# A gated cross-attention block with routed experts on one core: norms on GpSimd in wide operations, x resident from the load on, output bias added by TensorE

## Chip, core and metric

The kernel runs on 1 core of one Trainium2 chip. The metric is the device time in microseconds (us) of one execution. Engines: TensorE (PE, with its weight loads as PEld), VectorE (DVE), ScalarE (ACT), GpSimd (POOL), SyncE (SP, which issues DMAs). Each has its own instruction stream; streams meet only through semaphores, on which an engine waits in its own order.

## The reference

`x` and `ctx` are 128 batches of 64 tokens of 128 channels, all float32. Cut to what matters:

```python
def reference(x, ctx, g_xattn, g_ffn, W_q, b_q, W_k, b_k, W_v, b_v, W_o, b_o, w_red, wg, W1, b1, W2, b2):
    # xattn: 16 heads of 8 channels; softmax(q k^T / sqrt(8)) v, then @ W_o + b_o
    x = x + tanh(g_xattn[0]) * xattn(layernorm(x), ctx, ctx, ...)
    # ffn: 8 experts, hidden 256. logits = (h @ w_red) @ normed(wg).T; the expert
    # with the largest gate alone does gelu(h @ W1 + b1) @ W2 + b2, times its gate
    x = x + tanh(g_ffn[0]) * ffn(layernorm(x), w_red, wg, W1, b1, W2, b2)
    return x
```

`layernorm` has neither scale nor shift, eps is 1e-5.

## The kernel before

**Tiles.** The 8192 tokens are 64 units of 128 tokens (two batches). Four units make a step `s` (`CU` = 4, `NC` = 16 steps). The attention is one loop of 76 slots `k` (`SLOTS` = 64 + `LAGO`, `LAGO` = 12), which every engine walks in the same order of slots; slot `k` belongs to step `k // 4` at place `j = k % 4`. A unit passes through the slots with lags: its scores for the row maxima 4 slots behind (`LAG1`: L1121 on TensorE, then the two maxima, L976, on VectorE), the scores from which the exponentials are taken at lag 10 (`LAG2`: L1104 and L1111, then ScalarE's L596 and L598), sums and values at lag 11 (`LAGV`: L1184 and L1191), reciprocal (L982) and scaled rows (L993) on VectorE, and the output projection at lag 12 (L1195), added to the residual by L988. So in one slot TensorE does L1104, L1111, L1121, L1184, L1191, L1195, each for another unit.

**Once a step** TensorE turns the normed rows (L1263, `j` = 0) and the context (L1216, `j` = 0), makes keys (L1223, `j` = 1), queries (L1281, `j` = 2) and values (L1288, `j` = 3), and a product for the routing logits (L1207, `j` = 3). ScalarE copies each out of PSUM (L557 to L638). SyncE spreads keys and queries over partitions (L298, L305) and loads the context two steps and x three steps ahead (`next_loads`).

**x and the residual.** `XR` holds one record of 144 columns for each token: 128 of x (`X` is that part), 8 routing logits, the mean (`R_MEAN`), then 1/deviation (`R_RSTD`), gate (`R_GATE`) and row number (`R_ID`). x comes into three buffers `XC`. VectorE takes its statistics (L708, L716) into `mv`; `ve` is the variance plus eps. The output bias, tanh(gate) x (b_o + b_v W_o), is made in `bias_row` (VectorE, slot 2) as a row `tgbo` on all partitions, with its mean `bmean`. GpSimd writes x + `tgbo` into `X` (L367, `with_bias`), and mean + `bmean` into the record. What the bias does to the logits is `clog`, added for each group of units in `route_peak` (L809).

**GpSimd's step** has this order (L449 to L464): `spread` (L443, waits for ScalarE's turned maxima), records to send `before`, `norm` of step s+1 (power of -0.5 in `deviation`, L352; deviation, L360; four L375, one a unit; `with_bias`), `gate_norm` of step s-4 (L384, power L386, into the record), records to send `behind`. The power is taken for four columns at a time, once for each of the two norms. Steps 0 and 1 are normed by VectorE (L729), with the power on GpSimd.

**Routing** goes by `GROUPS` of units (12, 12, 12, 8, 8, 4, 4, 4). `route_slots` sets the slots of a group's six parts on VectorE; among them is the count on TensorE (L1158, L1161: one product with all columns of the group, then one for each unit with 8 columns fewer each time), and `route_place`, which waits for GpSimd's gate norm (`g_pay`). Records then go by indirect DMA (`send`, L400) to a table in HBM, sorted by expert; the number a step is written out in `sends`.

**Experts.** 71 tiles of 128 records: load (L320), norm (L948), turn (L1228), first product (L1236), gelu (L584), second product with its bias as a bfloat16 product over an exact three-part split (L1323, then L1326), gate and residual (L1037), and a scatter to the output by GpSimd (L471). The last group's four records are sent after the sixth scatter.

**Setup touched by the change.** `setup_gate` waits for `tgbo`; `setup_turn` turns it (L1083) and `setup_logits` makes from it `clog`, copied by ScalarE in `output_logits` (L550, L551) at slot 10; TensorE waits for `wox_ok` at slot 11. `split_biases` (L791 to L795) splits the experts' bias on VectorE at slot 10.

## Time and profile before

| what | before |
|---|---|
| time of three runs | 377.30, 378.38, 379.06 us, median 378.38 |
| span of the profiled execution | 376.4 us (first to last instruction); its own time is not listed apart, and stands as this span and what lies around it |
| PE / PEld busy | 332.6 us (88%) / 261.4 us (69%) |
| DVE / ACT / POOL busy | 290.0 us (77%) / 242.3 us (64%) / 266.9 us (71%) |
| chain that ended last | PE 62%, issue 9%, POOL 9%, DVE 8%, ACT 6% |
| mean granted TensorE clock | 0.963 of full speed |
| HBM | 17.13 MB read, 10.04 MB written, 72 GB/s |

Busy time is that in which an engine worked, waits left out. Matmuls are pipelined and their ends are modelled, so starts are the better guide on TensorE. Spans on POOL are rough. The chain is followed back from the last instruction to what released each step. The attention is over at about 265 us, the experts fill the rest.

### The profile page before, as it was taken

To read this page: it belongs to the slowest core of one execution; us is meant where nothing else is said; L and a number is where in the kernel's file an instruction comes from. 1 tells how busy PE (TensorE), PEld (TensorE's weight loads), DVE (VectorE), ACT (ScalarE), POOL (GpSimd) and SP (SyncE) were. 2 spreads that over 40 slices of the span, in tenths; PEclk is the share of its full clock that TensorE was granted. 3 is DMA by queue.
4 is the path that set the end of the run, shared out by engine and by line. 5 is a ranking of instruction groups with operands and counts; after the bars stand their busy time and mean duration, and the time that the engine had idled before them with its cause. 6 is when DMAs were issued, how large, how long until landed. Compare 5 with 4: busy or idle time off the path is not lost.

```text
span 376.4 us, 17275 instructions
## 1 busy us (share of the span) xinstructions
PE 332.6 (88%) x6654; PEld 261.4 (69%) x6654; DVE 290.0 (77%) x900; ACT 242.3 (64%) x604; POOL 266.9 (71%) x349
## 2 busy tenths in 40 slices
PE   3878999999999999999999997776888999999960
PEld 1534776776776777876876866655776899999950
DVE  7777788889899898989899799966578666666630
ACT  3747688788788788788788885644443455555520
POOL 6494664474685898798796876787557777777771
PEclk9978999999999999999999999997699999999995
DMA  5344334323313423323211121143014433333210
GB/s 114 105 141 141 102 95 129 111 80 98 118 48 98 139 80 105 95 70 102 71 63 51 44 93 50 41 129 97 36 56 132 137 120 99 114 110 100 66 46 0
DMA packets 47164, 34.13 MB, mean 91 GB/s; under 512 B 9800, under 2 KB 42955, under 8 KB 47083
## 3 DMA queue, kind: packets, MB, share of 16 engines
q1 hardware_dynamic: 42440, 23.90, 22.6%
q0 software_dynamic: 4352, 9.00, 6.6%
q8 instruction: 54, 0.88, 1.0%
q14 instruction: 26, 0.21, 0.2%
q10 hardware_dynamic: 292, 0.13, 0.1%
HBM read 17.13 MB, written 10.04 MB: 72 GB/s over the span
## 4 chain that ended last, share of the span: by engine, by line
PE 62%; issue 9%; POOL 9%; DVE 8%; ACT 6%; SPq 2%; DMA 1%; POOLq 0%; DVEq 0%; ACTq 0%
PE m L1326 10%; PE sc L1236 8%; PE pv L1184 7%; POOL records L400 6%; PE pv L1191 5%; PE sc L1111 5%; PE pv L1195 5%; PE m L1288 4%; PE sc L1121 3%; PE sc L1104 3%; PE sc L1228 2%; PE m L1323 2%; ACT PT L598 1%; PE m L1263 1%; PE m L1216 1%
## 5 line engine op out<-in xcount | busy, mean ns | idle before, releaser
L976 DVE TENSOR_REDUCE mx<-sc 128x8 f32<-128x512 f32 x128 | 82.2, 684 | 20.7 <-PE sc L1121 20.2
L471 POOL DMA_INDIRECT out<-fo,rr x71 | 70.0, 986 | 23.3 <-issue 19.3
L400 POOL DMA_INDIRECT records<-XR,pos x64 | 63.4, 991 | 20.4 <-issue 16.4
L982 DVE RECIPROCAL rec<-pv 128x128 f32<-128x128 f32 x64 | 61.1, 954 | 10.4 <-PE pv L1195 5.2
L596 ACT ACTIVATE PT<-sc 128x512 f32<-128x512 f32 x64 | 38.1, 595 | 28.2 <-issue 20.1
L1326 PE MATMUL m<-w,fgT 128*128 x284 | 50.7, 302 | 0.1
L1236 PE MATMUL sc<-fxT,w1s 128*128 128x128 f32 x284 | 45.6, 284 | 4.2 <-DVE w1s L964 3.3
L1037 DVE SCALAR_TENSOR_TENSOR fo<-m,rr 128x128 f32<-128x128 f32 x71 | 24.9, 350 | 29.8 <-PE m L1326 29.8
L1184 PE MATMUL pv<-PT,kz 128*32 128x128 f32 x1024 | 41.7, 281 | 6.5 <-DVE XR L988 5.9
L375 POOL TENSOR_SCALAR xn<-XC,mv,rstd 128x128 f32<-128x128 f32 x56 | 44.2, 799 | 0.0
L1236 PEld LDWEIGHTS sc<-fxT,w1s 128*128 128x128 f32 x284 | 38.6, 197 | 6.5 <-ACT fxT L578 4.2
L578 ACT ACTIVATE fxT<-sc 128x128 f32<-128x128 f32 x71 | 19.7, 278 | 35.4 <-PE sc L1228 35.4
L1191 PE MATMUL pv<-PT,V 128*32 128x64 f32 x2048 | 41.3, 220 | 0.2 <-issue 0.2
L1326 PEld LDWEIGHTS m<-w,fgT 128*128 128x128 f32 x284 | 38.0, 194 | 2.6 <-issue 0.4
L1111 PE MATMUL sc<-Qd,kT 32*128 32x128 f32 x1024 | 39.8, 270 | 0.0
L584 ACT ACTIVATE fgT<-sc 128x256 f32<-128x256 f32 x71 | 27.3, 384 | 18.7 <-PE sc L1236 18.3
L598 ACT ACTIVATE PT<-sc 128x512 f32<-128x512 f32 x64 | 38.3, 598 | 0.0
L1191 PEld LDWEIGHTS pv<-PT,V 128*32 128x32 f32 x2048 | 37.6, 111 | 0.3 <-issue 0.3
L1184 PEld LDWEIGHTS pv<-PT,kz 128*32 128x32 f32 x1024 | 24.5, 109 | 14.5 <-DVE XR L988 7.2
L1111 PEld LDWEIGHTS sc<-Qd,kT 32*128 32x128 f32 x1024 | 34.4, 186 | 0.0
L1195 PE MATMUL pv<-wox,OT 128*128 128x137 f32 x128 | 32.5, 336 | 0.0
L352 POOL TENSOR_TENSOR rstd<-ve,mhalf 128x4 f32<-128x4 f32 x16 | 16.5, 1034 | 21.6 <-DVE ve L721 21.4
(207 smaller groups left out, 681.3 us busy)
## 6 DMA issues: line engine op xcount, KB each, us to landing
rr<-records SPq DMA_DIRECT2D x71, 72.0 KB, 2.0
XC<-in_x SPq DMA_DIRECT2D x16, 256.0 KB, 3.2
C<-in_ctx SPq DMA_DIRECT2D x16, 256.0 KB, 3.1
Qd<-Qf SPq DMA_DIRECT2D x64, 64.0 KB
Kd<-kb SPq DMA_DIRECT2D x64, 32.0 KB
w<-in_L_ffn_W SPq DMA_DIRECT2D x16, 128.0 KB, 2.8
out<-fo,rr POOLq DMA_INDIRECT x71, 2.3
w1l<-in_L_ffn_W SPq DMA_DIRECT2D x8, 128.0 KB, 3.3
```

Source lines behind the costliest of these rows:

```text
L375: i = nc.gpsimd.tensor_scalar(xn[:, u, :], XC[c % 3][:, u, :], mv[c % 2][:, u, 0:1], rstd[:, u:u + 1], ALU.subtract, ALU.mult)
L400: nc.gpsimd.indirect_dma_start(out=records, out_offset=bass.IndirectOffsetOnAxis(ap=pos[:, u:u + 1], axis=0), in_=XR[:, u, :], in_offset=N ...
L471: nc.gpsimd.indirect_dma_start(out=out_rows, out_offset=bass.IndirectOffsetOnAxis(ap=rr[q][:, R_ID:R_ID + 1].bitcast(U32), axis=0), in_=fo ...
L598: nc.scalar.activation(pt[:, 2:4], sc[:, 2:4, 256:512], ACT.Exp).then_inc(pt_ok, 1)
L976: nc.vector.tensor_reduce(mx[c % 2][:, t:t + 2, HI * u:HI * u + HI], sc[:, t:t + 2, 0:256].rearrange("p t (i k) -> p t i k", i=HI), AX_X, ...
L982: nc.vector.reciprocal(rec[:, :], pv[:, P:2 * P]).then_inc(rec_ok, 1)
L1111: m = nc.tensor.matmul(sc[:, t, 256 + P * b:256 + P * b + P].rearrange("p (i q) -> p i q", i=2), kT[c % 3][r, u, b, :, :].rearrange("r l k ...
L1184: nc.tensor.matmul(pv[32 * t:32 * t + 32, P:2 * P].rearrange("p (b q) -> p b q", b=2), kz[:, 16 - 16 * i:48 - 16 * i], PT[n % 2][:, HI * t ...
L1191: last = nc.tensor.matmul(pv[32 * t:32 * t + 32, S * b:S * b + S], vf[:, at:at + 32], PT[n % 2][:, HI * t + 2 * b + i, :], start=False, st ...
L1195: last = nc.tensor.matmul(pv[:, 2 * P:2 * P + DX], OT[no % 2][:, :], wox[:, :], start=True, stop=True, skip_group_check=True)
L1236: i = nc.tensor.matmul(sc[:, 2 + p, P * m:P * m + P], w1s[p][:, P * m:P * m + P], fxT[p][:, :], start=True, stop=True, skip_group_check=True)
L1326: i = nc.tensor.matmul(o, fgT[p][:, m, :], w2[:, bass.ds(e, 1), m, :].rearrange("p o c -> p (o c)"), start=False, stop=(m == HH - 1), skip ...
```

## The change

- x is loaded straight into `X`; the buffers `XC` go, and statistics go straight into the record (`R_MEAN` and the column behind it).
- GpSimd's norm is two operations over all four units (subtract the mean, times 1/deviation) in place of four; `with_bias` and the two writes of the mean go.
- From step 4 on the two powers of a step are one over 8 columns (`roots`), ahead of the norm; the gate's result is copied into the record by an operation of its own. It now waits for the squares before the norm. In the last four steps, which have no norm, `roots` still takes a power and a copy.
- The bias is no longer added to x. `box` has 137 columns: the bias row and what it adds to the logits and the mean. VectorE splits it at slot 10 (`bias_parts`, behind ScalarE's `wox_ok`) into three bfloat16 rows at partitions 0, 32 and 64, and TensorE adds it with a bfloat16 product of 128 weights and 137 columns ahead of each L1195 (64 of them).
- `route_peak` loses the addition of `clog`; `bias_row` loses three of its four operations; SyncE's wait for `xb_ok` goes.

```diff
             def load_x(c):
-                sp.dma_start(XC[c % 3][:, :, :], x_t[:, CU * c:CU * c + CU]).then_inc(x_in[c % 3], 16)
+                sp.dma_start(X[:, CU * c:CU * c + CU, :], x_t[:, CU * c:CU * c + CU]).then_inc(x_in[c % 3], 16)
...
                 if s + 3 < NC:
                     sp.wait_ge(xn_ok, s + 1)
-                    sp.wait_ge(xb_ok, s + 1)
                     load_x(s + 3)
...
+            def root(c):
+                pool.wait_ge(ve_ok, c + 1)
+                nc.gpsimd.tensor_tensor(rstd, ve, mhalf[:, 0, :], ALU.pow).then_inc(rstd_ok, 1)
+
+            def roots(c, g):
+                pool.wait_ge(gsq_ok, CU * g + CU)
+                nc.gpsimd.tensor_scalar(gve, gsq[g % 2][:, :], 1.0 / D, EPS, ALU.mult, ALU.add).then_inc(gve_ok, 1)
+                if c is not None:
+                    pool.wait_ge(ve_ok, c + 1)
+                pool.wait_ge(gve_ok, g + 1)
+                if c is None:
+                    nc.gpsimd.tensor_tensor(inv[:, 1, :], gve, mhalf[:, 1, :], ALU.pow).then_inc(ginv_ok, 1)
+                else:
+                    nc.gpsimd.tensor_tensor(inv[:, :, :], both[:, :, :], mhalf[:, :, :], ALU.pow).then_inc(rstd_ok, 1)
+                    pool.wait_ge(rstd_ok, c + 1)
+                if c is None:
+                    pool.wait_ge(ginv_ok, g - (NC - 5) + 1)
+                nc.gpsimd.tensor_copy(XR[:, CU * g:CU * g + CU, R_RSTD], inv[:, 1, :]).then_inc(g_pay, 1)
...
             def norm(c):
+                r = slice(CU * c, CU * c + CU)
+                nc.gpsimd.tensor_tensor(xc[:, :, :], X[:, r, :], XR[:, r, R_MEAN:R_MEAN + 1].to_broadcast([P, CU, D]),
+                                        ALU.subtract).then_inc(xc_ok, 1)
                 deviation(c)
                 pool.wait_ge(xT_ps, c)
-                for u in range(CU):
-                    i = nc.gpsimd.tensor_scalar(xn[:, u, :], XC[c % 3][:, u, :], mv[c % 2][:, u, 0:1], rstd[:, u:u + 1],
-                                                ALU.subtract, ALU.mult)
-                i.then_inc(xn_ok, 1)
-                with_bias(c)
+                pool.wait_ge(xc_ok, c - 1)
+                nc.gpsimd.tensor_tensor(xn[:, :, :], xc[:, :, :], per_unit(rstd), ALU.mult).then_inc(xn_ok, 1)
...
                 if before:
                     send(sent, sent + before)
+                if s + 1 < NC and 1 <= s < 4:
+                    root(s + 1)
+                if s >= 4:
+                    roots(s + 1 if s + 1 < NC else None, s - 4)
                 if 2 <= s + 1 < NC:
                     norm(s + 1)
                 if s == 2:
                     constants()
-                if s >= 4:
-                    gate_norm(s - 4)
...
             def bias_row():
                 dve.wait_ge(bvo_ps, 1)
-                link(nc.vector.tensor_tensor(tgbo[:, :], m2[:, 128:128 + D], bo[:, :], ALU.add))
+                nc.vector.tensor_tensor(box[:, 0:D], m2[:, 128:128 + D], bo[:, :], ALU.add).then_inc(box_ok, 1)
                 dve.wait_ge(tg_ok, 1)
-                link(nc.vector.tensor_scalar(tgbo[:, :], tgbo[:, :], tg[:, 0:1], None, ALU.mult))
-                link(nc.vector.tensor_reduce(bmean[:, 0:1], tgbo[:, :], AX_X, ALU.add))
-                nc.vector.tensor_scalar_mul(bmean[:, 1:2], bmean[:, 0:1], 1.0 / D).then_inc(tgbo_ok, 1)
+
+            def bias_parts():
+                dve.wait_ge(wox_ok, 1)
+                link(nc.vector.tensor_copy(bpart[:, 0, :], box[:, :]))
+                link(nc.vector.tensor_tensor(brest[:, 0, :], box[:, :], bpart[:, 0, :], ALU.subtract))
+                link(nc.vector.tensor_copy(bpart[:, 1, :], brest[:, 0, :]))
+                link(nc.vector.tensor_tensor(brest[:, 1, :], brest[:, 0, :], bpart[:, 1, :], ALU.subtract))
+                link(nc.vector.tensor_copy(b3[:, :], brest[:, 1, :]))
+                link(nc.vector.memset(pick3[:, :].bitcast(U32), 0))
+                for r in range(3):
+                    i = nc.vector.memset(pick3[32 * r:32 * r + 1, :], 1.0)
+                i.then_inc(pick3_ok, 1)
+                for r in range(2):
+                    i = nc.vector.tensor_copy(b3[32 * r:32 * r + 32, :], bpart[32 * r:32 * r + 32, r, :])
+                i.then_inc(b3_ok, 1)
...
                 if k == 10:
                     split_biases()
+                    bias_parts()
...
-                link(nc.vector.tensor_tensor(e_, XR[:, f:l, D:D + NE], per_expert(clog[:, 0:NE], m), ALU.add))
-                nc.vector.tensor_reduce(c_[:, 0], e_, AX_X, ALU.max).then_inc(peak_ok, 1)
+                nc.vector.tensor_reduce(c_[:, 0], XR[:, f:l, D:D + NE], AX_X, ALU.max).then_inc(peak_ok, 1)
...
                 if 0 <= no < NU:
-                    last = nc.tensor.matmul(pv[:, 2 * P:2 * P + DX], OT[no % 2][:, :], wox[:, :], start=True, stop=True,
+                    if no == 0:
+                        pe.wait_ge(b3_ok, 1)
+                        pe.wait_ge(pick3_ok, 1)
+                    nc.tensor.matmul(pv[:, 2 * P:2 * P + DX], pick3[:, :], b3[:, :], start=True, stop=False,
+                                     skip_group_check=True)
+                    last = nc.tensor.matmul(pv[:, 2 * P:2 * P + DX], OT[no % 2][:, :], wox[:, :], start=False, stop=True,
                                             skip_group_check=True)
```

## Rows read from the trace of the kernel before

**Rows 1.** Busy time by stage: stretch, length, PE, PEld, DVE, ACT, POOL, clock, DMA.

```profile
60.00:200.00 140.00, 138.10 (x3663) 103.92 (x3651) 123.83 (x339) 116.37 (x271) 105.44 (x135) 1.00 0.31 92
220.00:258.00 38.00, 29.00 (x883) 22.80 (x881) 32.03 (x111) 22.26 (x61) 28.17 (x33) 1.00 0.29 86
```

**Rows 2.** Timeline, all engines (start, length, engine): L1263 of two steps, one ScalarE wait.

```profile
43.02 0.60 PE L1263 MATMUL m<-ident,xn 128*128 128x128 f32 x4
...
191.38 0.61 ACT L598 ACTIVATE PT<-sc 128x512 f32<-128x512 f32 x1
...
192.10 0.10 PEld L1104 LDWEIGHTS sc<-MD,usel 32*128 32x128 bf16 x4 [0.76 <-ACT PT L598]
...
198.18 0.60 PE L1263 MATMUL m<-ident,xn 128*128 128x128 f32 x4
```

**Rows 3.** Timeline of GpSimd in the expert stage: first record after the sixth scatter, last scatter.

```profile
280.01 0.96 POOL L400 DMA_INDIRECT records<-XR,pos  x1 [2.32 <-DVE XR L863]
...
367.69 0.98 POOL L471 DMA_INDIRECT out<-fo,rr  x1 [0.30 <-issue]
```

**Rows 4.** Timeline of TensorE in two second slots of a step; last, a group.

```profile
46.48 1.02 PE L1223 MATMUL m<-cT,wkp 128*128 128x512 f32 x2
...
47.44 0.29 PE L1104 MATMUL sc<-MD,usel 32*128 32x256 bf16 x4
...
187.21 0.50 PE L1195 MATMUL pv<-wox,OT 128*128 128x137 f32 x2
...
187.55 1.02 PE L1223 MATMUL m<-cT,wkp 128*128 128x512 f32 x2
...
188.45 0.50 PE L1161 MATMUL m<-oh,ones 128*128 128x96 bf16 x12
...
188.88 0.29 PE L1104 MATMUL sc<-MD,usel 32*128 32x256 bf16 x4
...
L1323 PE MATMUL m<-b2s,pick 128*128 x71 | 16.2, 227 | 0.1
```

**Rows 5.** Groups of GpSimd: out<-in, shapes, count | busy us, mean ns | idle before.

```profile
L375 POOL TENSOR_SCALAR xn<-XC,mv,rstd 128x128 f32<-128x128 f32 x56 | 44.2, 799 | 0.0
L367 POOL TENSOR_TENSOR XR<-XC,tgbo 128x512 f32<-128x512 f32 x16 | 20.3, 1270 | 0.0
...
L352 POOL TENSOR_TENSOR rstd<-ve,mhalf 128x4 f32<-128x4 f32 x16 | 16.5, 1034 | 21.6 <-DVE ve L721 21.4
...
L408 POOL TENSOR_TENSOR nrm<-nrm 8x1 f32<-8x1 f32 x1 | 1.5, 1481 | 1.1 <-DVE nrm L746 1.1
...
L354 POOL COPY XR<-mv 128x4 f32<-128x4 f32 x2 | 0.4, 192 | 0.0
```

**Rows 6.** Timeline at the end of the attention, and the stretch behind it.

```profile
253.13 0.19 DVE L809 TENSOR_TENSOR ex<-XR,clog 128x32 f32<-128x32 f32 x1
...
256.83 0.19 DVE L849 TENSOR_TENSOR ex<-ex,XR 128x32 f32<-128x32 f32 x1 [0.52 <-POOL XR L386]
...
259.48 1.08 PE L1184 MATMUL pv<-PT,kz 128*32 128x128 f32 x16 [2.17 <-DVE XR L988]
...
260.00:280.00 20.00, 17.35 (x144) 14.94 (x136) 12.65 (x51) 7.49 (x25) 11.62 (x13) 0.76 0.13 44
```

**Rows 7.** Timeline of VectorE, the bias row in slot 2: first and last of three.

```profile
17.67 0.29 DVE L754 TENSOR_SCALAR tgbo<-tgbo,tg 128x128 f32<-128x128 f32 x1
...
18.31 0.15 DVE L756 TENSOR_SCALAR bmean<-bmean 128x1 f32<-128x1 f32 x1
```

**Rows 8.** Timeline of slots 10 to 12: what the new split stands between.

```profile
37.33 0.20 ACT L551 ACTIVATE wox<-pv 128x9 f32<-128x9 f32 x1
37.35 1.29 DVE L976 TENSOR_REDUCE mx<-sc 128x8 f32<-128x512 f32 x2
...
38.67 0.60 ACT L598 ACTIVATE PT<-sc 128x512 f32<-128x512 f32 x1
...
39.95 0.29 PE L1104 MATMUL sc<-MD,usel 32*128 32x256 bf16 x4
...
41.42 0.32 PE L1121 MATMUL sc<-Kd,qb 32*64 32x256 bf16 x8 [0.73 <-issue]
```

91 lines of the change are left out of this document (34 added, 57 removed).

## The prediction

> **What bounds the kernel now.** I read busy time by stage first [rows 1], then one step of four units in order of time [rows 2], then the last stage. The reader should see three stages.
>
> From 60 to 200 us TensorE is busy 138.10 of 140 us at full clock (2.4 GHz), while VectorE has 16 us to spare and GpSimd 35 us [rows 1]. A step lasts (198.18 - 43.02) / 11 = 14.1 us [rows 2]. One place in a step is not TensorE's alone: at 192.10 the load of L1104 starts 0.11 us after ScalarE's second exponential ended (191.38 + 0.61), having waited 0.76 us for it, while the products of L1281 still ran [rows 2]. TensorE's 1.9 us of idle time in ten steps, 0.19 a step, is what such places leave.
>
> From 220 to 258 us there are no projections left. TensorE is busy 29.0 of 38 us and VectorE 32.0 [rows 1]. From about slot 69 on a loop sets the pace: values (TensorE), reciprocal and residual (VectorE), next values.
>
> In the expert stage GpSimd sets the end: from the last group's first record at 280.01 to the last scatter at 367.69 there are 4 records and 71 - 6 = 65 scatters, 87.7 us over 68 intervals, 1.29 us each, with only issue time between them [rows 3]. The change touches none of these. So whatever moves the start of the expert stage moves the end by as much.
>
> **The change, part by part.** The sum is made against the profiled execution, whose span is 376.4 us (the page's first line); the runs shown have 378.38 us as their median, 2.0 us more, and I add that at the end.
>
> *1. The bias product (TensorE), 64 instructions added.* Each unit gets a bfloat16 product, 128 weights by 137 columns, between L1191 and L1195. No row shows it there, so I bound it:
> - From below: the slot at 187.55 has a count (one product of 96 columns and twelve of 96 falling to 8, 720 columns in all) behind L1223, that at 46.48 has none. L1223 to L1104 takes 188.88 - 187.55 = 1.33 us against 47.44 - 46.48 = 0.96 us, so 13 products cost 0.37 us, 0.028 us each, or 0.51 ns a column [rows 4]. By the column, 137 columns cost 0.07 us; by the instruction alone 0.03 us. I take 0.03 as the end of the range.
> - From above: L1195 is a float32 product with the same 137 columns in two passes, 187.21 to 187.55, so 0.17 us a pass [rows 4]. The nearest relative is L1323, also bfloat16, 128 by 128, and followed by float32 products: 16.2 us over 71 is 0.228 us of overlapped duration [rows 4], which is no spacing; I take the pass's 0.17 as the end.
> I take 0.08 us, just over the price by the column, since that row has real bfloat16 weight loads, hidden as these should be. A negative price is excluded: nothing is taken off TensorE.
>
> Slots 12 to 63 make 13 steps. In each, the product of the slot that ends in the ScalarE wait is hidden by the 0.19 us above; three count: 39 x 0.08 = 3.1 us. Were that cover gone, 13 x 0.08 = 1.0 us more. In slots 64 to 69 VectorE sets the pace and covers it. In the last six the loop contains it: 6 x 0.08 = 0.5 us. Sum +3.6 us; ends 39 x 0.03 + 0.2 = 1.4 us and 52 x 0.17 = 8.8 us.
>
> *2. GpSimd.* Before, a step takes four L375 at 0.80, L367 at 1.27 and two powers at 1.03 [rows 5]: 6.5 us. After: two products of 128x512, both at L367's 1.27 us, one power of 128x8, and one small copy at 0.19, as L354 [rows 5]. The power of eight columns isn't shown: four columns take 1.03 us, and one column over 8 partitions took 1.48 us [rows 5], so it doesn't go by columns; I take 1.1 us, with 2.1 us (two old ones) as the other end. After is 3.8 us, 2.7 us a step less. It is worth nothing: GpSimd has 35 us to spare in those 140 us [rows 1]. Even at 2.1 us, and with the new wait for the squares of the gate's norm, which now stands ahead of the step's norm, the normed rows are needed only in the next step. Queued behind that new wait are the norm and the second batch of records; the waited-for squares belong to the step's first slot, over 10 us before TensorE needs the rows.
>
> In the last steps there is no norm left, and the separate copy into the record makes GpSimd slower, 0.2 to 0.3 us a step with its wait. There it matters once: at 256.83 VectorE waited 0.52 us for GpSimd's gate norm [rows 6]. Two copies lie ahead, +0.5 us, but VectorE's own slots are later by as much through part 1. I count 0.1.
>
> Here a rule speaks against the change. The rows show a one-input operation over 128 columns at 0.80 us and a two-input one over 512 at 1.27 us [rows 5]: wide wins, 2.5 us for 3.2. The Trainium skill (GPSIMD Engine Reference, Engine selection) has it that a one-input operation runs roughly at line rate on GpSimd, and a two-input one about twice as slow as on VectorE; by it the old norm would be the cheaper and GpSimd's load would not fall. The measured rows decide for me, and the sum is the same by either, since this work is covered.
>
> *3. VectorE.* The three operations of the bias row that go (L754 to L756, 17.67 to 18.46) lie on the way to the row maxima of the second unit: -0.8 us [rows 7]. Against that, splitting the bias comes at slot 10: five linked operations over 137 columns at about 0.29 us, as L754 [rows 7], then six small ones (between 0 and 6 x 0.29; I take 0.7): 2.2 us. It must wait for ScalarE's L551 (37.33 + 0.20), which falls just at the time the maxima of slot 11 started (37.35) [rows 8]. Those move by 2.4 us. Behind them stand ScalarE's exponentials, which ended at 38.67 + 0.60 and would now end at 41.7, and TensorE's slot 12, which started at 39.95 and so is 1.7 us late; 0.73 us of it disappears in the wait that L1121 had at 41.42 [rows 8]. So +0.9 us; ends 0 and 2.4. The addition of the logits' constant goes from each group; three of these lie in the stage where VectorE paces, -0.19 each [rows 6], of which two count: -0.4 us.
>
> *4. Loads.* x goes straight into the resident rows, in pieces of the same 512 bytes; SyncE loses one wait, for rows that TensorE doesn't need yet: 0. What covers it is the three steps of lead.
>
> **Sum.** +3.6 (product) + 0.1 (copy) - 0.8 + 0.9 - 0.4 = +3.4 us: span 379.8, time 381.8 us. A difference under 0.5% (1.9 us) is about what a measurement of this kernel can't tell from no change; the limits are 376.5 and 380.3 us.
>
> **The rivals.**
> - *The product nearly disappears* (0.03 us as the short ones, more cover than I count). For: a weight load can run beside the product before it, as L1104's does [rows 2], and 13 products cost 0.37 us [rows 4]. Against: those were short. 39 x 0.03 + 0.2 = 1.4, and the other terms at -0.2: +1.2 us, 379.6 us. Chance 0.22.
> - *The product costs more* (0.12 us) and the setup's stall counts fully. 39 x 0.12 + 6 x 0.12 = 5.4 us, with the stall at its end of 2.4 (+0.1 - 0.8 + 2.4 - 0.4 = +1.3): +6.7 us, 385.1 us. For: the float32 product behind it must load its weights beside a shorter one. Against: twelve loads of 128 weights among the count's products cost no more than their columns [rows 4]. Chance 0.18.
> - *Faster: TensorE's clock stays up at the change of stage.* Place: slots 73 to 75, where L1184 waited 2.17 us for VectorE at 259.48, and the granted clock then fell to half (1.2 GHz). Its mean over 260 to 280 us is 0.76, which makes 20 x 0.24 x 2 = 9.6 us at half clock [rows 6]. If this idle time is broken up, TensorE, busy 17.35 of those 20 us, gets back at most 9.6 x 0.87 / 2 = 4.1 us. It decides only if the rest of the sum is under 4.1 - 1.9 = 2.2 us, so with the cheap product: 378.4 + 1.2 - 4.1 = 375.5 us. Against: the wait comes from GpSimd's late gate norm and register loads, which the change doesn't shorten. Chance 0.08. The same clock can also fall once more, at slot 11, where TensorE now idles 1.7 us longer; that belongs to the case before.
> - *It doesn't do what it says*, GpSimd isn't relieved (the power takes 2.1 us, broadcast operands are slow). Then POOL rows show it and the time doesn't, being covered. No chance of its own.
>
> **How the numbers follow.** Forecast as summed 0.52; cheap product 0.22 (within 0.5%); dear product 0.18; clock 0.08 (faster). Slower: 0.52 + 0.18 = 0.70, same 0.22, faster 0.08. The range from 377.8 to 385.5 us takes in the cheap product and most of the dear one, and leaves out the clock's case and the far end of 8.8 us. The likeliest case's own range is 380.3 to 383.5 us.
>
> **What would show it.** Right: the period of a step, by the starts of L1263, goes from 14.1 to 14.3 or 14.4 us; TensorE still over 98% busy from 60 to 200 us; the new product's start lies 0.08 us before L1195's; GpSimd's busy time falls by some 40 us with nothing gained; the maxima of slot 11 start 2 us later; from the last group's records to the end 87.7 us as before. Wrong: a step still of 14.1 us (then the product is free), a step under 14 us (then something I hold for covered was on the path), or a clock row near 1.0 between 260 and 270 us.

## The result, and the profile of the changed kernel

The changed kernel takes 385.98 us (median of 4 runs, 384.15 to 388.53), the kernel before beside it 378.53 us (377.30 to 379.06). The ratio is 1.0216, 95% interval 1.0161 to 1.0271: slower, by 7.5 us where the prediction had 3.4 us, and 385.98 lies just above its range, which ended at 385.5. The profiled execution has a span of 384.9 us against 376.4, so 8.5 us are to be found. The ratios leave out executions more than 1.5% above the fastest of their kernel, mostly those of the variants in the fourth set of experiments below (nine of 24 of two of them) and of the kernel before in the fifth (ten of 17), so there the medians of all executions stand beside them.

First the busy time by stage, the answer to [rows 1] and to the stretch of [rows 6] (columns as there).

```profile
60.00:200.00 140.00, 135.62 (x3580) 102.69 (x3580) 122.85 (x322) 112.64 (x262) 71.35 (x89) 0.99 0.31 93
220.00:258.00 38.00, 32.94 (x973) 26.00 (x966) 33.01 (x102) 25.45 (x66) 25.98 (x32) 1.00 0.18 61
260.00:280.00 20.00, 14.35 (x289) 11.80 (x281) 13.04 (x48) 10.31 (x31) 15.12 (x19) 0.91 0.30 88
```

GpSimd has its relief: 71.35 us of 140 in place of 105.44. TensorE, which sets the pace there, is not busier but idler: 135.62 us in place of 138.10. A product that cost much would have kept it busy. So something makes it wait. (The later stretches lie some 10 us earlier in the work than those of the kernel before.)

Next the start of the steps, by the first transpose of each (L1279, before L1263). This table takes both traces' timelines of TensorE; the lengths are those of the stretch that ends with this start (so the expectations below count steps), and the last column shows where the time goes.

| start of step | before, us | after, us | length up to it, before | the same, after | later than before |
|---|---|---|---|---|---|
| 2 | 28.79 | 28.52 | 12.27 | 11.63 | -0.27 |
| 3 | 43.02 | 48.06 | 14.23 | 19.54 | +5.04 |
| 7 | 99.16 | 104.58 | 14.04 | 14.10 | +5.42 |
| 8 | 113.25 | 121.39 | 14.09 | 16.81 | +8.14 |
| 9 | 127.36 | 136.53 | 14.11 | 15.14 | +9.17 |
| 11 | 155.94 | 165.84 | 14.54 | 15.09 | +9.90 |
| 14 | 198.18 | 209.12 | 14.09 | 15.09 | +10.94 |
| 15 | 212.78 | 223.50 | 14.60 | 14.38 | +10.72 |

Most lengths are 14.09 or 14.10 us, 0.06 more than the 14.03 or 14.04 of before. The loss comes in a few lumps: 5.3 us up to the start of step 3, 2.7 up to step 8, 1.0 up to steps 9 and 14, and 0.6 up to step 11. At the end it is 8.5 us, so 2.2 us are gained back behind the start of step 15.

**The first lump.** The timelines of VectorE, of GpSimd and of TensorE in slots 10 to 12 of the changed kernel, the answer to [rows 8].

```profile
35.88 2.81 DVE L803 CAST bhl<-bw 128x8 bf16<-128x8 f32 x1
38.72 0.17 DVE L804 TENSOR_TENSOR br<-bw,bhl 128x8 f32<-128x8 f32 x1
...
39.42 0.38 DVE L757 CAST bpart<-box 128x137 bf16<-128x137 f32 x1
...
41.35 0.62 DVE L764 MEMSET pick<- 1x128 bf16 x3
42.01 0.40 DVE L767 COPY b<-bpart 32x137 bf16<-32x137 bf16 x2
42.43 1.29 DVE L987 TENSOR_REDUCE mx<-sc 128x8 f32<-128x512 f32 x2
```

```profile
35.84 1.04 POOL L388 TENSOR_TENSOR xn<-xc,inv 128x512 f32<-128x512 f32 x1
36.81 0.20 POOL L415 MEMSET tri<- 128x128 bf16 x1
...
38.56 0.10 POOL L423 MEMSET ebase<- 128x1 f32 x1
38.61 0.16 POOL L424 IOTA tile_i<- 128x36 int32 x1
```

```profile
44.41 0.29 PE L1115 MATMUL sc<-MD,usel 32*128 32x256 bf16 x4 [4.30 <-ACT PT L600]
```

The maxima of slot 11 start at 42.43 in place of 37.35. Of the 5.1 us, 3.0 are the new pieces of the bias (39.42 to 42.41). The rest comes from the first copy of the *old* split of the expert biases: eight columns to bfloat16, 2.81 us, where the same copy took 0.15 us before; the four instructions behind it are 0.7 us shorter in sum than they were beside the old norm. It starts 0.04 us behind GpSimd's second wide product of the norm, and ends at 38.69, when the last of GpSimd's 22 memsets (38.56 + 0.10) is over. Nothing that it reads is late. Behind it TensorE waits 4.30 us for ScalarE, and the granted clock then falls to half (1.2 GHz) for a while: its mean is 0.72 over 44 to 50 us, 1.00 before. So the 5.3 us hold the wait and the slow stretch behind it.

**The second lump.** VectorE and GpSimd where group 0 is placed.

```profile
113.41 0.86 DVE L856 TENSOR_TENSOR ky<-ky,oh 128x96 f32<-128x96 f32 x1
114.30 0.25 DVE L858 TENSOR_REDUCE pos<-ky 128x12 uint32<-128x96 f32 x1
114.47 2.13 DVE L860 TENSOR_TENSOR ex<-ex,XR 128x96 f32<-128x96 f32 x1
116.52 1.27 DVE L987 TENSOR_REDUCE mx<-sc 128x8 f32<-128x512 f32 x2
```

```profile
113.11 1.04 POOL L388 TENSOR_TENSOR xn<-xc,inv 128x512 f32<-128x512 f32 x1
114.11 2.38 POOL L394 TENSOR_TENSOR w<-w,w1l 128x1024 f32<-128x1024 f32 x1
```

Both routing instructions read two tiles in SBUF. They took 0.26 and 0.25 us before; here one ends just behind GpSimd's product (114.27 and 114.15), and the other with its subtraction on w1 at 116.5. The reduction between them, with one tile, keeps its 0.25 us. TensorE then waits 1.95 us for ScalarE, until 118.48, and the clock is 0.72 over 119 to 125 us, which is the lump up to step 9. Those up to steps 11 and 14 hold the same pair of instructions at 0.91 and 0.97 us, beside the norm alone.

What did the kernel before do at that hour? These are its rows, with the norm in its old form:

```profile
107.94 0.26 DVE L845 TENSOR_TENSOR ky<-ky,oh 128x96 f32<-128x96 f32 x1
...
108.40 0.25 DVE L849 TENSOR_TENSOR ex<-ex,XR 128x96 f32<-128x96 f32 x1
```

```profile
106.07 3.24 POOL L375 TENSOR_SCALAR xn<-XC,mv,rstd 128x128 f32<-128x128 f32 x4
...
111.83 2.38 POOL L392 TENSOR_TENSOR w<-w,w1l 128x1024 f32<-128x1024 f32 x1
```

They stood beside GpSimd's norm then too, and lost nothing; the subtraction came 3 us behind them. None of the routing's two-tile instructions (L818, L828, L845, L849) fell beside a GpSimd instruction of 512 or more columns in that trace. This gives **theory G**: GpSimd's work was covered as far as its own deadlines go, but it holds up VectorE's instructions of some forms while it runs, and the change gave it new forms and new hours. Within it, **theory W** says that the form of the norm matters and not only the hour. **Theory P** is the prediction's: the products, and the split's own time, make the loss. The Trainium skill ("SBUF — State Buffer", Who interferes with whom) has a rule for G: a VectorE instruction with two SBUF inputs contends with a GpSimd instruction that reads SBUF, as does a copy or cast in a two-port mode, and whoever comes first holds the shared pair for its whole instruction. L860 beside L394 agrees with it to 0.1 us; it is weighed once more below.

**GpSimd's groups**, the answer to [rows 5].

```profile
L366 POOL TENSOR_TENSOR inv<-both,mhalf 128x8 f32<-128x8 f32 x11 | 18.2, 1657 | 14.8 <-DVE both L720 13.9
L383 POOL TENSOR_TENSOR xc<-XR 128x512 f32<-128x512 f32 x14 | 14.6, 1043 | 0.0
L388 POOL TENSOR_TENSOR xn<-xc,inv 128x512 f32<-128x512 f32 x14 | 14.6, 1039 | 0.0
...
L370 POOL COPY XR<-inv 128x4 f32<-128x4 f32 x16 | 3.0, 189 | 1.0
```

**The product** in the changed kernel, between the values (L1202) and the output projection, the answer to [rows 4]:

```profile
185.78 0.62 PE L1202 MATMUL pv<-PT,V 128*32 128x64 f32 x31
186.34 0.23 PE L1209 MATMUL pv<-b,pick 128*128 128x137 bf16 x1
186.41 0.45 PE L1211 MATMUL pv<-wox,OT 128*128 128x137 f32 x2
```

**The end.** First record of the last group and last scatter, the answer to [rows 3]:

```profile
288.47 0.96 POOL L402 DMA_INDIRECT records<-XR,pos  x1 [1.48 <-DVE XR L874]
...
376.18 0.98 POOL L473 DMA_INDIRECT out<-fo,rr  x1 [0.30 <-issue]
```

376.18 - 288.47 = 87.7 us, as before.

### The profile page after: what moved, and what is told of

It is laid out like the page before. It is cut to its first block, busy times and chain, and to the rows that moved or that the text cites. A ratio compares the mean times of both kernels' runs of the same rounds, so it can differ in the third digit from the quotient of the medians.

```text
span 384.9 us, 17329 instructions
## 1 busy us (share of the span) xinstructions
PE 335.6 (87%) x6718; PEld 264.5 (69%) x6718; DVE 297.9 (77%) x900; ACT 242.7 (63%) x604; POOL 225.1 (58%) x292
## 4 chain that ended last, share of the span: by engine, by line
PE 56%; DVE 12%; issue 11%; POOL 9%; ACT 6%; SPq 2%; DMA 1%; POOLq 0%; DVEq 0%; ACTq 0%
PE m L1342 10%; PE sc L1252 8%; POOL records L402 6%; PE pv L1195 6%; PE pv L1202 5%; PE sc L1122 5%; PE pv L1211 3%; PE sc L1132 3%; PE m L1304 3%; PE sc L1115 2%; DVE mx L987 2%; PE m L1339 2%; PE sc L1244 2%; PE m L1279 2%; PE m L1232 2%
## 5 line engine op out<-in xcount | busy, mean ns | idle before, releaser
L443 POOL TENSOR_TENSOR MD<-mS,imask 128x256 bf16<-128x256 bf16 x16 | 9.7, 608 | 76.8 <-ACT mS L647 76.8
L1195 PE MATMUL pv<-PT,kz 128*32 128x128 f32 x1024 | 42.4, 283 | 6.7 <-DVE XR L998 6.3
L1202 PE MATMUL pv<-PT,V 128*32 128x64 f32 x2048 | 42.1, 223 | 0.0
L1122 PE MATMUL sc<-Qd,kT 32*128 32x128 f32 x1024 | 39.8, 271 | 0.0
L1202 PEld LDWEIGHTS pv<-PT,V 128*32 128x32 f32 x2048 | 38.4, 113 | 0.1
L1195 PEld LDWEIGHTS pv<-PT,kz 128*32 128x32 f32 x1024 | 24.9, 110 | 15.1 <-DVE XR L998 7.3
L1115 PEld LDWEIGHTS sc<-MD,usel 32*128 32x128 bf16 x256 | 6.6, 91 | 39.1 <-ACT PT L600 26.4
L1115 PE MATMUL sc<-MD,usel 32*128 32x256 bf16 x256 | 18.4, 278 | 15.1 <-ACT PT L600 14.4
```

Of the source, the lines that this page charges most:

```text
L1115: nc.tensor.matmul(sc[:, t, 256:512].rearrange("p (b i q) -> p i b q", b=2, i=2), usel[r, u, :, :].rearrange("r l k -> r (l k)"), MD[c % 2 ...
L1122: m = nc.tensor.matmul(sc[:, t, 256 + P * b:256 + P * b + P].rearrange("p (i q) -> p i q", i=2), kT[c % 3][r, u, b, :, :].rearrange("r l k ...
L1195: nc.tensor.matmul(pv[32 * t:32 * t + 32, P:2 * P].rearrange("p (b q) -> p b q", b=2), kz[:, 16 - 16 * i:48 - 16 * i], PT[n % 2][:, HI * t ...
L1202: last = nc.tensor.matmul(pv[32 * t:32 * t + 32, S * b:S * b + S], vf[:, at:at + 32], PT[n % 2][:, HI * t + 2 * b + i, :], start=False, st ...
```

## The experiments

Eighteen runs were made, in five sets (the expectations call a set a "call"): the changed kernel itself twice, five repeats of other variants, and eleven more. The kernels of a set ran on one chip, beside the kernel before. **Two kinds of chip answered.** In two sets the kernel before took 377.5 and 378.3 us, with a clock of 0.96 in the profiled runs of the variants. In three it took 463.2, 464.5 and 467.6 us: there TensorE was granted 0.88 to 0.91, falling for long stretches from about 118 us on. On those the times say little, but the first 110 us of the traces, and the single instructions, read as elsewhere.

### First set: one part at a time (clock 0.88 to 0.91)

*No products.*

```diff
-                    nc.tensor.matmul(pv[:, 2 * P:2 * P + DX], pick3[:, :], b3[:, :], start=True, stop=False,
-                                     skip_group_check=True)
-                    last = nc.tensor.matmul(..., OT[no % 2][:, :], wox[:, :], start=False, stop=True,
+                    last = nc.tensor.matmul(..., OT[no % 2][:, :], wox[:, :], start=True, stop=True,
```

> The changed kernel with the bias product of each unit left out (64 small products fewer; the output bias and its logits are then missing from the result, all else stays). Theory P, the prediction's own: each product costs TensorE 0.06 to 0.08 us where it waits for nothing, so the kernel loses 3.5 to 4 us: 386.0 to about 382.3, ratio to the kernel before 1.010. Theory G, formed from the two traces (the slots of the changed kernel have the product in an opening that was already there; the loss lies in VectorE instructions held up while GpSimd works): about 0.02 us a unit, so -0.5 to -1.5 us, about 385, ratio 1.018; the step of four units goes from 14.09 to 14.03 us.

*Subtractions on w1 one step earlier.*

```diff
-                if 6 <= s < 8:
-                    fold_bias(s - 6)
+                if 5 <= s < 7:
+                    fold_bias(s - 5)
```

> The changed kernel with the two subtractions over half of w1 (GpSimd, 2.38 us each) one step earlier, in steps 5 and 6 in place of 6 and 7. Theory G: in the changed kernel the second of them runs at 114.1 to 116.5, over VectorE's routing instruction of group 0 that reads two tiles in SBUF, which takes 2.13 us there and 0.25 in the kernel before, and TensorE then waits 1.95 us and its clock falls; a step earlier no such instruction of VectorE is due. It expects that instruction below 1.0 us, no fall of the clock at 120 to 123 us and 2.5 to 3.5 us off the kernel: about 383, ratio 1.012. Theory P (the products and the split make the loss, GpSimd's work is covered): no change, within 0.5 us of the changed kernel, ratio 1.021.

*Constants one step later.*

```diff
-                if s == 2:
+                if s == 3:
                     constants()
```

> The changed kernel with GpSimd's constants (some 20 memsets and iotas, about 2.9 us) one step later, in step 3. Theory G: VectorE's first copy of the expert biases to bfloat16 in slot 10 takes 2.81 us because it starts while these memsets run back to back; without them beside it it takes 0.15 to 1.0 us (1.0 if it still starts within GpSimd's wide product of the norm), the maxima of slot 11 start at 39.8 to 40.6 in place of 42.43, and the kernel is 2 to 3 us shorter: about 383.5, ratio 1.013. Rival D (what is long there is the chain of bias pieces of VectorE itself, and the copy waits for data, the load of the expert biases): the copy ends at the same time, the maxima start at 42.4 and the time stays at 386, ratio 1.021.

*The norm in its old form.*

```diff
-                nc.gpsimd.tensor_tensor(xc[:, :, :], X[:, r, :], ..., ALU.subtract).then_inc(xc_ok, 1)
                 deviation(c)
                 pool.wait_ge(xT_ps, c)
-                pool.wait_ge(xc_ok, c - 1)
-                nc.gpsimd.tensor_tensor(xn[:, :, :], xc[:, :, :], per_unit(rstd), ALU.mult).then_inc(xn_ok, 1)
+                for u in range(CU):
+                    i = nc.gpsimd.tensor_scalar(xn[:, u, :], X[:, CU * c + u, :], XR[:, CU * c + u, R_MEAN:R_MEAN + 1],
+                                                rstd[:, u:u + 1], ALU.subtract, ALU.mult)
+                i.then_inc(xn_ok, 1)
```

> The changed kernel with the old form of the norm on GpSimd (four tensor_scalars of 0.80 us in place of two wide instructions of 1.04 us), all else as changed. Theory W (the form itself matters: instructions with two tiles in SBUF as inputs hold VectorE up, those with one tile and two columns do not): the routing instructions that took 0.8 to 1.0 us take 0.25 to 0.3 wherever only the norm ran beside them, and the kernel is 0.5 to 2 us shorter, about 385, though GpSimd works 1.1 us a step longer. Theory G without W (what counts is when GpSimd works, in either form): the long ones move to other places, time 385.5 to 387.5. Theory P: no change.

**Measured.** The kernel before took 463.19 us. The four took 470.40, 471.41, 470.03 and 471.45 us; ratios 1.0143 (1.0079 to 1.0208), 1.0164 (1.0101 to 1.0226), 1.0157 (1.0082 to 1.0232) and 1.0153 (1.0076 to 1.0230). By time they tell nothing apart: the interval of the first holds P's 1.010 and G's 1.018. By their rows they do:

- Without the products, the lengths up to steps 5, 6 and 7 are 14.03, 14.03 and 14.04 us; with them, where the subtractions or the constants were moved, 14.09 or 14.10. So a product costs 0.06 / 4 = 0.015 us, as G has it.
- With the subtractions moved, the routing instruction takes 0.25 us, and the length up to step 8 is 14.32 us in place of 16.81. The clock stays at 1.00 behind it, as G has it; but on such a chip it does so in the unedited changed kernel too, so that part is not shown here.
- With the constants moved, the first copy takes 1.02 us, and the maxima of slot 11 start at 39.79. G had 1.0 us and 39.8 to 40.6.
- With the norm in its old form, both routing instructions and the copy are short, though GpSimd's norm runs over them (113.20 to 116.33, and 35.22 to 38.34): W. But now the bias's second copy falls beside the memsets and takes 1.67 us, so the maxima of slot 11 start at 42.19 all the same.
- Rival D, that the first copy waits for its data, falls: with the constants moved it has ended by 36.24 us and with the old norm by 36.29, where the changed kernel's ended at 38.69.

Start times differ between runs by more than these gains, so the stall is better read as the distance from the maxima of slot 10 to those of slot 11. It is 3.03 us in the kernel before; 8.02 in the changed kernel, 6.37 and 7.24 in its two repeats below; 6.04 or 6.05 in all four runs with the constants moved and the pieces in slot 10; and 3.03 or 3.04 in the four below with the constants moved and the pieces elsewhere. So the pieces cost 3.0 us, and the copy held beside the memsets between 0.3 and 2.0 more. The distance is the same 6.05 in the two runs with only the constants moved, whether the first copy takes 1.02 us (here) or 0.25 (its repeat in the fourth set), since VectorE then waits 0.71 us for ScalarE's `wox`.

Timeline of VectorE in these kernels (subtractions moved; constants moved, then its repeat; old norm):

```profile
115.15 0.25 DVE L860 TENSOR_TENSOR ex<-ex,XR 128x96 f32<-128x96 f32 x1
```

```profile
35.22 1.02 DVE L803 CAST bhl<-bw 128x8 bf16<-128x8 f32 x1
...
39.79 1.29 DVE L987 TENSOR_REDUCE mx<-sc 128x8 f32<-128x512 f32 x2
```

```profile
37.29 0.25 DVE L803 CAST bhl<-bw 128x8 bf16<-128x8 f32 x1
...
39.07 0.23 DVE L757 CAST bpart<-box 128x137 bf16<-128x137 f32 x1 [0.71 <-ACT wox L553]
```

```profile
36.14 0.15 DVE L803 CAST bhl<-bw 128x8 bf16<-128x8 f32 x1
...
114.48 0.24 DVE L856 TENSOR_TENSOR ky<-ky,oh 128x96 f32<-128x96 f32 x1
...
114.93 0.38 DVE L860 TENSOR_TENSOR ex<-ex,XR 128x96 f32<-128x96 f32 x1
```

### Second set: the kernel unedited, the other direction, and sums (clock 0.89 to 0.91)

*The changed kernel again*, unedited:

> The changed kernel itself again, as the measure for the runs beside it, since the first four kernels ran on a chip that granted TensorE less clock (0.88 to 0.91 in place of 0.96) and took 467 to 474 us. Where the chip grants 0.96 again, every theory expects 386 us and a ratio to the kernel before of 1.021; where it grants 0.88, about 472 us and 1.016 to 1.021, by the ratios of 1.014 to 1.016 of its four variants there.

*The kernel before, with its split moved beside the memsets:*

```diff
-                if k == 10:
+                if k == 11:
                     split_biases()
```

> The kernel before with one edit: VectorE splits the expert biases in slot 11 in place of slot 10, so that the split falls beside GpSimd's memsets of the constants (39.37 to 42.3 us). Theory G (a copy of VectorE that starts beside GpSimd's work from SBUF or memsets waits for it): one of the split's five instructions takes 1 to 3 us in place of 0.15 to 0.38, the maxima of slot 12 start 1.5 to 3 us later than the 41.80 of the kernel before, and the kernel is 0 to 2.5 us longer, ratio 1.000 to 1.007. Theory P (the split costs its own 1.6 us wherever it stands, GpSimd's work is covered): each instruction keeps 0.15 to 0.38 us, ratio 1.000.

*Subtractions and constants both moved* (the two edits of the first set):

> The changed kernel with both moves of GpSimd's work that the first call looked at one by one: the constants one step later, the two subtractions on w1 one step earlier. Theory G: VectorE's first copy of the split takes 1.0 us in place of 2.8 and the routing instruction of group 0 takes 0.25 in place of 2.13 us; against the changed kernel beside it 3.5 to 6 us less, ratio to the kernel before 1.006 to 1.012. Theory P: the same time as the changed kernel.

*Everything but the constants:* old norm, subtractions moved, and VectorE's own pieces taken apart; `bias_parts` now takes the columns it works on.

```diff
+            link(nc.vector.memset(pick3[:, :].bitcast(U32), 0))      (behind norm(1), ahead of the slots)
...
+                if k == 4:
+                    bias_parts(slice(0, D), box_ok)
                 if k == 10:
-                    split_biases()
-                    bias_parts()
+                    bias_parts(slice(D, DX), wox_ok)
+                if k == 13:
+                    split_biases()
```

> The changed kernel with everything that theory G would do to it: the norm on GpSimd in its old form of four tensor_scalars with one tile as input (the one power a step stays), the subtractions on w1 one step earlier, the bias's first 128 columns split in slot 4 and only its 9 logit columns in slot 10, the selector written before the slots, the expert biases split in slot 13. Theory G: no instruction of VectorE in the routing above 0.5 us, the maxima of slot 11 at 37 to 38 us in place of 42.4, steps of 14.03 to 14.1 us; 7.5 to 10 us less than the changed kernel, ratio to the kernel before 0.995 to 1.002. Theory P (three to four of the lost microseconds are the products): ratio 1.007 to 1.012.

**Measured.** The kernel before took 464.54 us. The changed kernel: 470.76, ratio 1.0132 (1.0055 to 1.0208). The kernel before with its split moved: 466.75, 1.0008 (0.9969 to 1.0047). The two moves: 470.26, 1.0103 (1.0061 to 1.0145). Everything but the constants: 469.91, 1.0078 (1.0026 to 1.0130). The order is G's, but neighbours lie within each other's intervals, and the sizes are not G's: the two moves are 0.5 us under the changed kernel where G had 3.5 to 6, and the last one's ratio lies in P's range of 1.007 to 1.012 and above G's, which ended at 1.002.

The move in the kernel before is a miss for G. It expected one of the five instructions at 1 to 3 us; the first took 0.40 us in place of 0.15, though it stood in the row of memsets:

```profile
39.28 0.40 DVE L791 CAST bhl<-bw 128x8 bf16<-128x8 f32 x1
```

But later in the same run a thing happened that the kernel before had not shown: the routing instruction of group 2 fell beside its wide addition L367, and took 1.42 us, while its neighbour beside the norm took 0.34. VectorE, then GpSimd:

```profile
217.08 0.34 DVE L845 TENSOR_TENSOR ky<-ky,oh 128x96 f32<-128x96 f32 x1
...
217.63 1.42 DVE L849 TENSOR_TENSOR ex<-ex,XR 128x96 f32<-128x96 f32 x1
```

```profile
214.53 3.14 POOL L375 TENSOR_SCALAR xn<-XC,mv,rstd 128x128 f32<-128x128 f32 x4
217.64 1.26 POOL L367 TENSOR_TENSOR XR<-XC,tgbo 128x512 f32<-128x512 f32 x1
```

In groups 0 and 1 of this run the same instruction took 0.25 and 0.38 us beside the norm. So it is no matter of the changed kernel's code: in the kernel before, too, what GpSimd does beside it makes it long or short.

The short first copy shows that a copy beside the memsets need not wait for all of them. In the changed kernel's profile the same copy took 2.81 us, in its two repeats 1.31 and 2.02. What decides how soon it gets in is open. With it varies the first lump: step 4 starts at 62.3, 59.7 and 62.5 us in the three. And in the last of the four the nine logit columns were in the wrong place: in slot 10 they waited 1.69 us for ScalarE and then stood beside the constants, with one copy of nine columns at 1.85 us, so the maxima of slot 11 were no earlier (42.69):

```profile
39.58 0.18 DVE L761 CAST bpart<-box 128x9 bf16<-128x9 f32 x1 [1.69 <-ACT wox L553]
...
40.00 1.85 DVE L763 CAST bpart<-brest 128x9 bf16<-128x9 f32 x1
```

### Third set: the whole, on a chip at 0.96

*The changed kernel again:*

> The changed kernel itself once more, beside the three below. Two chips so far granted TensorE 0.88 to 0.91 and gave ratios of 1.013 (0.9055 clock). Every theory expects 1.021 where the chip grants 0.96 and 1.013 where it grants 0.90.

*All moves:* as the last one above, with the constants in step 3 and the nine columns in slot 11 in place of 10.

> The changed kernel with the norm of four tensor_scalars, the subtractions on w1 one step earlier, the constants one step later, the bias's first 128 columns split in slot 4, its 9 logit columns in slot 11, the expert biases in slot 13, the selector written before the slots. The last run of this kind had the 9 columns in slot 10, where VectorE waited 1.7 us for ScalarE and 1.85 us beside the constants. Theory G: no such wait is left, the maxima of slot 11 start at 36 to 37 us, the fourth step starts (first transposes) at 41 to 43 us against 44.7 to 48.1 in the changed kernel; at a clock of 0.96 the kernel takes 7.5 to 10 us less than the changed one (ratio to the kernel before 0.995 to 1.002), at 0.90 some 3 to 6 us less (1.000 to 1.006). Theory P: 1.008 to 1.012 at either clock.

*The same without the products:*

> The kernel above without the 64 bias products (output bias and its logits missing from the result). The pair prices the products with no stall of VectorE in the way. Theory G: a step is 14.03 in place of 14.09 us where the clock is whole, so the kernel is 0.5 to 1.5 us shorter than the one above. Theory P (0.06 to 0.08 us each): 3.5 to 4.5 us shorter, steps of 13.8 us or less against the one above.

*GpSimd's three moves alone* (old norm, subtractions earlier, constants later), VectorE as changed:

> The changed kernel with GpSimd's three moves alone (four tensor_scalars for the norm, subtractions on w1 one step earlier, constants one step later); VectorE's bias pieces stay in slot 10 as changed. Theory G: every routing instruction below 0.5 us and the expert bias copies at 0.15 us each, the maxima of slot 11 at 39 to 40 us because of the pieces' own 3.0 us, 1 to 2.5 us longer than the kernel with all moves. Theory P: the time of the changed kernel.

**Measured**, beside the kernel before at 377.47 us:

| kernel | us, median | ratio (95%) | span, us |
|---|---|---|---|
| changed | 388.01 | 1.0289 (1.0216 to 1.0363) | 387.1 |
| GpSimd's three moves | 381.76 | 1.0114 (1.0042 to 1.0187) | 381.4 |
| all moves | 378.96 | 1.0056 (1.0022 to 1.0090) | 376.9 |
| all moves, no products | 379.56 | 1.0060 (1.0029 to 1.0091) | 378.1 |

GpSimd's moves give 6.2 us back, VectorE's another 2.8 (G had 1 to 2.5): 9.0 us, where G expected 7.5 to 10. The ratio of 1.0056 is nobody's: G had 0.995 to 1.002, P 1.008 to 1.012, and the changed kernel itself took 2 us more here than in its first measurement. Two other marks of G were missed by 2 to 3 us: the maxima of slot 11 start at 39.59 in place of 36 to 37 and the fourth step at 45.01 in place of 41 to 43 (the next set takes up why), and GpSimd's moves alone have their maxima at 41.85 in place of 39 to 40. The products are still there in the third row; the pair prices them. The lengths up to steps 5 to 14 of the kernel with all moves are 14.09 to 14.18 us, the four with lumps included. TensorE is busy 98.45 of 100 us from 110 to 210:

```profile
110.00:210.00 100.00, 98.45 (x2636) 74.46 (x2632) 88.90 (x248) 82.51 (x193) 68.13 (x88) 1.00 0.27 86
```

From the start of step 3 to that of step 15 it is 170.55 us with them and 169.71 without, 0.84 us over 48 products: 0.018 us each, where P had 3.5 to 4.5 us in all. The times do not even show the 0.84, 378.96 with and 379.56 without. In the two profiles what undoes it is at the change of stage. The stretch of the kernel with the products, then that of the one without:

```profile
255.00:275.00 20.00, 15.07 (x246) 12.76 (x239) 13.36 (x52) 9.30 (x30) 15.15 (x19) 0.91 0.23 71
```

```profile
255.00:275.00 20.00, 15.48 (x209) 13.40 (x197) 12.25 (x47) 8.43 (x27) 14.29 (x18) 0.74 0.25 74
```

In each of eight profiles at 0.96 (this set, the last, and the first two kernels) the clock over 255 to 275 us is either 0.91 or 0.74, and from the start of step 15 to the last group's first record it takes 64.9 to 65.0 us with the one (changed kernel, its repeat, all moves) and 66.6 to 67.2 with the other (kernel before and the four others). That is the 2.2 us which the changed kernel gained behind step 15. What picks one or the other is open. Among the five at 0.74 the kernel before is the longest with 67.2 us, the four variants take 66.6 to 67.1, so little else in this stretch has changed.

### Fourth and fifth set: the single moves, and a better placing

In the kernel with all moves, step 2 started at 30.65 us, 2.1 later than in the changed kernel: the pieces in slot 4 (20.37 to 22.17) stand right ahead of the maxima that start at 22.21. VectorE has idle time ahead of the maxima of slots 8 and 9, so:

```diff
-            link(nc.vector.memset(pick3[:, :].bitcast(U32), 0))      (and the three rows; now in slot 8)
...
-                if k == 4:
+                if k == 7:
                     bias_parts(slice(0, D), box_ok)
```

> The kernel with all moves (378.96 us, ratio 1.0056) with the bias's first 128 columns split in slot 7 in place of 4 and the selector written in slot 8 in place of ahead of the slots; VectorE waited 1.7 to 2.3 us for TensorE there. Theory G: the third step starts at 28.4 to 29 us in place of 30.65 and the kernel is 1 to 2.5 us shorter than the one before it, 376.5 to 378, ratio 0.998 to 1.003: level with the kernel before, whose own end it may pass by a little. Rival C (what is gained at the start is given back because TensorE's clock falls elsewhere): ratio 1.005 to 1.007 as before.

The three single moves again, edits as in the first set:

> The edit of e2_fold again (subtractions on w1 in steps 5 and 6), where the clock is whole. Theory G: routing instruction of group 0 at 0.25 us in place of 2.13, the eighth step 14.1 to 14.5 us in place of 16.8, and no half clock at 120 to 123 us; 2.5 to 3.5 us less than the changed kernel's 386 to 388, ratio 1.013 to 1.019. Rival (the wait is filled by another): 386 to 388.

> The edit of e3_const again (constants in step 3), where the clock is whole. Theory G: the first copy of the split at 1.0 us in place of 2.0 to 2.8, the third step 16.5 us in place of 19.5 to 19.9; 1 to 3 us less than the changed kernel, ratio 1.014 to 1.023.

> The edit of e4_unitnorm again (norm of four tensor_scalars), where the clock is whole. Theory W: no routing instruction of groups 0 to 2 above 0.5 us, steps 8, 9, 11 and 14 at 14.1 to 14.6 in place of 16.8, 15.1, 15.1 and 15.1; 3.5 to 5.5 us less than the changed kernel, though GpSimd works 16 us more, ratio 1.008 to 1.016. Theory G without W (only the hour of the work counts, not the form): within 1.5 us of the changed kernel.

**Measured**, fourth set: the chip granted 0.89 to 0.91 again, the kernel before took 467.63 us. The four took 468.87, 473.74, 475.49 and 472.71 us, ratios 0.9987 (0.9939 to 1.0036), 1.0126 (1.0069 to 1.0184), 1.0164 (1.0105 to 1.0223) and 1.0053 (1.0006 to 1.0101). By the medians of all executions the first is 1.003 and the last 1.011. By their rows: better placing, the third step starts at 28.68 us, as G has it; subtractions moved, the routing instruction 0.25 us and 14.32 us up to step 8, both as G has it; constants moved, the first copy 0.25 us where G had 1.0, and 17.83 us up to step 3 where it had 16.5. Two were repeated:

> The kernel with all moves and VectorE's bias pieces in slots 7, 8 and 11, again, where the clock is whole. In the last call its eighth step began at 112.9 us, against 113.25 in the kernel before's profile and 116.0 in the kernel with pieces in slot 4. Theory G: ratio to the kernel before 0.995 to 1.001, 1.5 to 3 us less than the 378.96 of the kernel with the pieces in slot 4. Rival C (given back elsewhere): 1.004 to 1.007.

> The changed kernel with the norm of four tensor_scalars alone, again, where the clock is whole. Theory W: steps 8, 9, 11 and 14 at 14.1 to 14.6 us, 3.5 to 5.5 us less than the changed kernel's 386 to 388, ratio 1.008 to 1.016. Theory G without W: 1.018 or more.

**Measured**, fifth set, clock 0.96, kernel before 378.32 us (372.38 to 379.93): all moves, better placed, 378.55 us (375.69 to 380.55), ratio 1.0070 (1.0023 to 1.0117); old norm alone, 383.65 us (381.22 to 384.90), ratio 1.0213 (1.0136 to 1.0290). By the medians of all executions these are 1.001 and 1.014. The first is 0.4 us under the 378.96 of the pieces in slot 4, where G had 1.5 to 3 us, and its ratio of 1.0070 is rival C's: G missed. The second is W's 1.008 to 1.016 by the medians only; its ratio lies in the range given to G without W (1.018 or more).

The old norm by itself takes 2.3 us off the 385.98 of the changed kernel, or 4.4 off its repeat in the third set (in whose profile 2.1 us more lay in the expert stage). These compare kernels of different sets; W had 3.5 to 5.5. So the time alone does not settle it. The trace shows more than the time: from the start of step 7 to that of step 15 it takes 113.43 us, the changed kernel 118.92 and the kernel before 113.62. **To restore the norm's form is enough to take away all of the loss in the middle of the run.** The lengths up to steps 8, 9, 11 and 14 are 14.17, 14.15, 14.17 and 14.17 us, within W's 14.1 to 14.6. The subtraction on w1 still runs right behind the norm, but 1.1 us later, since the norm lasts 3.12 us, and VectorE is past by then (GpSimd, then VectorE, old norm alone):

```profile
112.08 3.12 POOL L386 TENSOR_SCALAR xn<-XR,inv 128x128 f32<-128x128 f32 x4
115.17 2.37 POOL L394 TENSOR_TENSOR w<-w,w1l 128x1024 f32<-128x1024 f32 x1
```

```profile
113.81 0.38 DVE L860 TENSOR_TENSOR ex<-ex,XR 128x96 f32<-128x96 f32 x1
```

No edit but the norm's form separates the two kernels, so this is shown, though not how much of the 2.7 us up to step 8 is the form and how much the subtraction's later hour; up to steps 11 and 14 the norm is the only wide instruction beside the routing. Of these 5.5 us, 1.8 were given back at the change of stage, whose clock was 0.74 here (66.7 us in place of 65.0). The first lump stays (18.96 us up to step 3): the copies stand beside the memsets as before, one at 1.49 us, and the bias's pieces are still there.

The better placing brings the start of step 8 to 112.9 us in the fourth set, 0.4 ahead of the kernel before, and 114.8 in the fifth (step 2 started 1.4 us later there). No version was measured clearly faster than the kernel before: the best is level with it by the medians (378.55 against 378.32), behind it by the ratio there, and level by the ratio of the fourth set.

## Why the prediction was wrong

The direction was right and its reason was not, so the direction was luck: of the sum's +3.4 us the products made +3.6, and they cost about 1. By its own steps:

- **The sum of part 2 failed, and with it the forecast.** "It is worth nothing: GpSimd has 35 us to spare" asked whether GpSimd's work is in time. It did not ask what GpSimd's instructions do to VectorE's beside them, nor how many microseconds their hour moves. The durations were close enough: 1.04 us for a wide product where 1.27 was taken, 1.66 for the power of eight columns, between the 1.1 taken and the end of 2.1. The wide norm held up the routing instructions and brought the subtraction over them: 5.3 us from step 7 to step 15 (118.92 - 113.62, some 0.5 of it the products), priced at zero, with no end kept for the range. The trace of before shows the routing's instructions unharmed beside the old norm, and never beside a wide instruction of GpSimd; what no row showed was put at nothing.
- **The stall at slot 10** had the right place and mechanism, and the wrong size. The pieces were put at 2.2 us and took 3.0 (39.42 to 42.41), mainly since three memsets of one row took 0.62 us and the two copies 0.40. Not in the sum at all was the old split's first copy, which grew by 2.7 us and moved what follows it by 2.0. The maxima moved by 5.1 us and not 2.4, and of this nothing disappeared: the length up to step 3 grew by 5.3 us, the end of the term being 2.4 (its own +0.9 is 1.7 less 0.73, so rather 1.0). The fall of the clock that the text put to "the case before" came.
- **The product** was the wrong term that carried the forecast: 0.08 us each, +3.6 in all. It measured 0.018 us (0.015 by the steps without it), below the lower end of 0.03. The start of the projection is 0.07 us behind it, as foretold, but what follows the projection starts 0.28 us behind that (186.41 to 186.69) where it took 0.34 before (187.21 to 187.55), so nearly all of the 0.07 is gone again. So the rival of the cheap product was true, and its verdict "the same" was not, because the other terms were not at -0.2.
- **The rival on the clock** also came about in part: 0.91 over 260 to 280 us in place of 0.76, and 2.2 us gained from step 15 to the records, where at most 4.1 was given. Its doubt was that the change doesn't shorten the wait; the wait of TensorE there even grew, from 2.17 to 2.87 us, and the clock stayed up all the same.
- **The bias row** gave 0.3 us at the start of step 2 by these two profiles, where 0.8 was taken; but that start lies at 28.1 and 28.4 us in the changed kernel's repeats, and between 26.5 and 30.1 in variants whose edits come later, so neither figure is shown.
- **The last stage's two small terms** (+0.1 and -0.4) cannot be told from the clock's part in it.
- **The signs to look for.** GpSimd's busy time fell by 41.8 us (266.9 to 225.1; 40 was foretold), and the expert stage took its 87.7 us: right. "TensorE still over 98% busy" failed at 96.9%, and a step of "14.3 or 14.4 us" at 14.09. "Wrong: a step still of 14.1 us (then the product is free)" is what the trace shows.

The Trainium skill's rule quoted in the prediction (GPSIMD Engine Reference, Engine selection: one-input operations at line rate, two-input ones slow) would have made the old norm the cheaper. The rows say otherwise for GpSimd's own time (3.12 us for the old form against 2.08 for the new), and the sum was "the same by either". From step 7 to step 15 the kernel sided with the old form nevertheless (113.43 us against 118.92), for a reason which is in neither.

In numbers, from the profiles: -0.3 (start) + 5.3 (slots 10 to 12: 3.0 the pieces, the rest the held copy) + 5.3 (the norm's form and the hour of the subtraction, with some 0.5 of products) + 0.4 (from step 3 to step 7, the products in it) = +10.7 us at step 15, and - 2.2 at the change of stage: 8.5 us.

## What to carry to other kernels

An engine with time to spare is not free to be rearranged: before an edit to GpSimd's instructions is counted at nothing, list VectorE's instructions beside their new hours, and look for those that read two tiles in SBUF or copy and cast within it; where the trace shows no such instruction beside one of the new form, keep an end for it in the range. One-off work put ahead of a loop's maxima is paid by everything behind it: put it in a slot in which the engine waits, and check in the timeline that its own inputs are there by then. Where the clock can fall, price a small change from the starts of steps at whole clock, and not from the total.
